# Whole gate and silu bursts on ScalarE in a scan kernel: where each stands among the decays

## The chip, the cores and the metric

One core of one Trainium2 chip runs the whole program. The metric is device time in microseconds (us), the median of several executions; 0.5% of it is 2.4 us.

## What is computed

A selective scan, four batches of 512 positions, 512 channels, 16 states, then a mixed linear layer. Cut to what matters:

```
x   = silu(causal_conv4(ctx @ in_proj.T) + conv_b)             # u, per batch 512 channels x 512 positions
dt  = softplus(dt_proj(x_proj(x)[:16]) + dt_b);  B, C = the other 32 rows of x_proj(x)
state = state * exp(dt * A) + (dt * x) * B      # a recurrence along the positions, 16 states
y   = sum_n(state * C) + D * x
x1  = x_in + y * silu(layernorm(x_in))           # the gate
out = x1 + layernorm(x1) @ sum_r(factors) / sqrt(8) + bias     # the FFN
```

## The kernel before

The work is 16 steps, `s` = 0 to 15: batch `b` = s // 4 and a block of 128 channels `k` = s % 4. A step has eight pairs `j` = 0 to 7, each two of the 16 states over 512 positions. A pair is written (s,j) below. Four engines work on a pair in turn:

- ScalarE (ACT) writes the decays exp(dt*A) of the pair into `dA`, two activations of 128x512 (`decay`, line 786). `dA` lies in PSUM and has two places, so the decays of pair j wait until pair j-2 has left its place (`decays`, just below it).
- GpSimd (POOL) writes dtu*B into `h`, a ring of eight pairs (`times_b`, line 1103), and at the end of a step `dtu` of the next one (line 1089).
- VectorE (DVE) scans the pair (`scan`, line 956) and multiplies by C (`times_c`, line 962). For the pairs that the table `POOL_C` names, the scan writes into `h`, not `dA`, and POOL multiplies, three pairs later (line 1096).
- TensorE (PE) adds the two states into `y` in PSUM (`state_sum`, line 528), in the order of `SUM_ORDERS`.

The order on each engine is written out by hand in `step(s)`: after the decays of pair j, ACT does whatever tables name slot j. ACT keeps one table set, for exp and ln. Softplus and silu need another, so each such burst is a table load, the work, and a load back. Softplus of the next step stands at `SOFTPLUS_SLOTS[s]`. The gate of a batch, four silu activations of 128x512 (line 700), is done in its first step in two halves at `GATE_SLOTS[b]`. The silu of the next batch's convolution, which writes `u` (line 692), is done in two pieces behind pair 4: three blocks in the second step of a batch, one in the third. `STATS_SLOTS` places two activations on layer norm statistics (lines 704, 710). `t_final_` (line 774) copies a finished FFN tile out of PSUM, `t_xnT_` (line 770) a transposed tile, both when PE has made them.

On DVE, `gate_y` (line 970) gates the previous step's y behind scan 1, `add_x1` (line 998) adds it to x1 behind scan 2 or 3, and three `conv_part`s (line 930) stand behind scans 6, 7 and 0 for blocks not convolved by PE.

Of the kernel before, what the change touches and what calls it, by code (L numbers as in the profile page):

```python
# [27 lines left out]
ACT = mybir.ActivationFunctionType  # L28
# [4 lines left out]
BATCH, L, DM = 4, 512, 256  # L33
DI, N, TAPS, RANK = 512, 16, 4, 16
KB = DI // P
# [21 lines left out]
TENSOR_CONV = (5, 6, 7, 8, 9)  # L57
SUM_ORDERS = {(0,): (1, 0, 2, 3, 4, 5, 6, 7), (0, 2): (1, 0, 3, 2, 4, 5, 6, 7), (0, 2, 4): (1, 0, 3, 2, 5, 4, 6, 7),
              (0, 4): (1, 0, 2, 3, 5, 4, 6, 7)}
POOL_C = ((0, 4), (0,), (0, 2), (0, 2), (0, 2), (0, 2), (0, 2), (0, 2, 4), (0, 2), (0, 2, 4), (0, 2), (0, 2, 4), (0, 2),  # L60
          (0, 2), (0, 2), (0, 2))
SOFTPLUS_SLOTS = (2, 2, 2, 2, 0, 2, 2, 2, 0, 2, 2, 2, 0, 2, 2, 2)
GATE_SLOTS = ((4, 6), (2, 5), (2, 5), (2, 5))
C_LAG = 3
STATS_SLOTS = (5, 3, 5, 3, 3, 3, 3, 3, 3, 3, 3, 3, 3, 3, 3, 3)
TENSOR_RESIDUAL = (0, 1, 2, 6, 8)
FIRST_FILL = (6, 0, 2, 2, 3)
IDLE_FILL = {(0, -1): 14, (0, 3): 3, (1, 3): 4, (3, 3): 4, (4, 1): 3, (5, 6): 2, (7, 6): 2, (8, 1): 2, (8, 6): 2, (9, 6): 2,
# [3 lines left out]
def build(nc, x, ctxT, w_inT, channel, x_projT, dt_wT, factors, bias, out):  # L72
    bc_dram = nc.dram_tensor("bc_scratch", (BATCH, 2 * N, L), F32, kind="Internal").ap()

    with ExitStack() as ctx:
# [33 lines left out]
        u = sb("u", [P, 2, KB, L])  # L109
        acc = sb("acc", [P, KB, L])  # L110
# [119 lines left out]
        def blocks_at(part, s, at):  # L230

            early = {t: ((t + KB, 5), (t + KB, 6), (t + KB, 7), (t + KB + 1, 1), (t + KB + 1, 4),
                         (t + KB + 2, -1), (t + KB + 2, 2)) for t in range(2 * KB)}
            for t in (KB - 2, 2 * KB - 2):
                early[t] = early[t][:FINAL] + ((t + KB + 2, 3),)
            early[KB - 1] = early[KB - 1][:EVAC] + ((2 * KB, 5),) + early[KB - 1][LAYER:]
            early[2 * KB - 1] = early[2 * KB - 1][:LAYER] + ((3 * KB, 5), (3 * KB + 1, 1))
            if part <= NORM:
                early.update(RAW_STATS)
            return [t for t, parts in early.items() if parts[part] == (s, at)]  # L240
# [418 lines left out]
        def _(act):  # L659
# [23 lines left out]
                act.wait_ge(conv, conv_count(k))  # L683
                act.activation(u[:, 0, k, :], acc[:, k, :], ACT.Silu).then_inc(u_done, 1)

            def silu_blocks(b, first, last):

                wait_conv(act, b * KB + last - 1)
                if b >= 2:
                    act.wait_ge(y_init, (b - 1) * KB)  # L690
                    act.wait_ge(d_dtu, (b - 1) * KB)
                act.activation(u[:, b % 2, first:last], acc[:, first:last], ACT.Silu).then_inc(u_done, last - first)

            def gate_half(b, half):

                act.wait_ge(g_nb, (b + 1) * KB)
                if b > 0:
                    act.wait_ge(gated, b * KB - 1 + half)
                for k in range(half * (KB // 2), (half + 1) * (KB // 2)):
                    act.activation(gate[:, k, :], x1_block(b, k), ACT.Silu, bias=g_r[:, 2, k:k + 1],  # L700
                                   scale=g_r[:, 1, k:k + 1]).then_inc(g_done, 1)

# [97 lines left out]
            def step(s):  # L800
                b, k = divmod(s, KB)

                nu = s + KB + 2
                is_u, is_g, is_d = nu < STEPS, b + 1 < BATCH, s + 1 < STEPS

                for j in range(PAIRS):
                    decays(s, k, j)

                    if s == KB + 1 and j in SCALE_SLOTS:
                        i = SCALE_SLOTS.index(j)  # L810
                        act.wait_ge(f_centred, i + 1)
                        act.activation(fsum[:, i, :], fsum[:, i, :], ACT.Copy, scale=FR ** -0.5).then_inc(f_scaled, 1)

                    if j == SOFTPLUS_SLOTS[s] and is_d:
                        act.preload_act_table_set("softplus")  # L815
                        softplus(s + 1)
                        act.preload_act_table_set("natural_log_exp_and_others")  # L817
                    if s == 0 and j == 0:
                        conv_tap(work0, KB)
                    if s == 0 and j == 1:  # L820
                        x_in_copy(work1, KB + 1)
                        lnv(g_r, g_mv, slice(0, KB), g_aggr, KB, g_lnv)
                        expv(g_r, slice(0, KB), g_lnv, 1, g_expv)
                        act.wait_ge(g_neg, 1)
                        for i in range(KB):
                            nb(g_r, g_mv, i, g_expv, 1, g_nb)
                    if s == KB and j == 7:
                        act.wait_ge(f_mean, 1)
                        act.activation(row_b[:], work1[:], ACT.Copy).then_inc(f_mean_evac, 1)
                    for t in blocks_at(FINAL, s, j):  # L830
                        t_final_(t)
                    if s == 0 and j == 5:
                        conv_out(KB + 1)
                    if j == 3 and s > 0 and s + KB + 1 in TENSOR_CONV:
                        conv_out(s + KB + 1)
                    if j == STATS_SLOTS[s] and is_g:
                        act.wait_ge(x_landed, (b + 2) * 16)
                        act.wait_ge(g_nb, (b + 1) * KB)
                        minus_mean(g_mv, b + 1, k, g_scratch, g_mean)
                    if j == 3 and s - 1 in TENSOR_RESIDUAL:  # L840
                        x1_evac(s - 1)
                    if k == 0 and j in GATE_SLOTS[b]:
                        act.preload_act_table_set("silu_and_others")
                        gate_half(b, GATE_SLOTS[b].index(j))
                        act.preload_act_table_set("natural_log_exp_and_others")
                    if j == 4 and k in (1, KB - 2) and b + 1 < BATCH:
                        act.preload_act_table_set("silu_and_others")
                        silu_blocks(b + 1, *((0, KB - 1) if k == 1 else (KB - 1, KB)))
                        act.preload_act_table_set("natural_log_exp_and_others")
                    if j == STATS_SLOTS[s] and is_g:  # L850
                        var_sum(g_mv, b + 1, k, g_scratch, g_mean, s + 1, g_var)
                    if j in (2 if s == STEPS - 1 else 4 if s == STEPS - 2 else 6 if s == STEPS - 3 else 5, 7):
                        for w in w_at(s)[j // 7:j // 7 + 1]:
                            w_copy(w)
                    for t in blocks_at(EVAC, s, j):
                        if is_g:
                            act.wait_ge(g_var, s + 1)
                        t_xnT_(t)
                    for t in blocks_at(MEAN, s, j):
                        act.wait_ge(x1_added, (t // KB + 1) * KB)  # L860
                        if t > 2 * KB:
                            act.wait_ge(t_var, t)
                        elif t > 0:
                            act.wait_ge(t_turned, t)
                        minus_mean(t_mv, t // KB, t % KB, xn[:], t_mean)
                    for t in blocks_at(VAR, s, j):
                        var_sum(t_mv, t // KB, t % KB, xn[:], t_mean, t + 1, t_var)
                    for t in blocks_at(NORM, s, j):
                        lnv(t_r, t_mv, slice(t % KB, t % KB + 1), t_var, t + 1, t_lnv, 1.0 / DI)
                        if t >= 2 * KB and t % KB == 0:  # L870
                            act.wait_ge(t_xn, 2 * KB)
                        expv(t_r, slice(t % KB, t % KB + 1), t_lnv, t + 1, t_expv)
                        if t >= 2 * KB:
                            continue
                        nb(t_r, t_mv, t % KB, t_expv, t + 1, t_nb)
                        t_xn_(t)
                    if j == 6 and k == KB - 1 and is_g:
                        lnv(g_r, g_mv, slice(0, KB), g_var, (b + 1) * KB, g_lnv, 1.0 / DI)
                        expv(g_r, slice(0, KB), g_lnv, b + 2, g_expv)
                        for i in range(KB):  # L880
                            nb(g_r, g_mv, i, g_expv, b + 2, g_nb)
                    if j == 6:
                        if is_u and nu in TENSOR_CONV:
# [350 lines left out]
```

## Time and profile before

| | |
|---|---|
| median of 3 runs | 481.11 us (479.55 to 481.75) |
| the profiled execution | 481.48 us, of which the profile's span is 479.7 us |
| TensorE clock granted, mean | 0.979 |
| PE / DVE / ACT / POOL busy | 91 / 94 / 76 / 90% of the span |
| chain that ended last, by engine | POOL 39%, DVE 18%, issue 18%, PE 15%, DMA 5%, ACT 3% |

The busy shares tell how much an engine works, not whether it is waited for. The chain names at each moment one engine that released the next work. The waits tell which engine sat idle until which other one was done.

### The profile page before, as it was taken

To read this page: it belongs to the slowest core of one execution; us is meant where nothing else is said; L and a number is where in the kernel's file an instruction comes from. 1 tells how busy PE (TensorE), PEld (TensorE's weight loads), DVE (VectorE), ACT (ScalarE), POOL (GpSimd) and SP (SyncE) were. 2 spreads that over 40 slices of the span, in tenths; PEclk is the share of its full clock that TensorE was granted. 3 is DMA by queue.
4 is the path that set the end of the run, shared out by engine and by line. 5 is a ranking of instruction groups with operands and counts; after the bars stand their busy time and mean duration, and the time that the engine had idled before them with its cause. 6 is when DMAs were issued, how large, how long until landed. Compare 5 with 4: busy or idle time off the path is not lost.

```text
span 479.7 us, 4156 instructions
## 1 busy us (share of the span) xinstructions
PE 438.1 (91%) x1119; PEld 187.4 (39%) x1132; DVE 451.2 (94%) x324; ACT 363.0 (76%) x595; POOL 429.4 (90%) x226
## 2 busy tenths in 40 slices
PE   8998798899999779899989798899989998989996
PEld 5242342434433243433434243343434443334432
DVE  5798899999999999999999997999998999999996
ACT  4678795887689798796899879697899876654422
POOL 4369999899999999997999979798999969999982
PEclk9999899999999969999999889999999999999999
DMA  5799746339992000100793000000495000000002
GB/s 193 260 350 359 198 81 142 51 78 217 292 362 77 1 0 0 53 15 0 239 412 122 0 23 0 1 23 0 118 396 237 1 22 23 22 22 22 2 0 88
DMA packets 16848, 53.97 MB, mean 113 GB/s; under 512 B 1828, under 2 KB 2084, under 8 KB 15800
## 3 DMA queue, kind: packets, MB, share of 16 engines
q1 hardware_dynamic: 15384, 45.14, 26.3%
q0 software_dynamic: 1152, 8.39, 8.7%
q8 instruction: 9, 0.15, 0.1%
q10 hardware_dynamic: 288, 0.18, 0.1%
q14 instruction: 15, 0.12, 0.1%
HBM read 49.24 MB, written 4.46 MB: 112 GB/s over the span
## 4 chain that ended last, share of the span: by engine, by line
POOL 39%; DVE 18%; issue 18%; PE 15%; DMA 5%; ACT 3%; SPq 2%; POOLq 0%; DVEq 0%
POOL h L1103 30%; DVE dA L956 12%; POOL h L1096 6%; PE y L528 6%; DMA b_rep<-bc_scratch 4%; DVE h L956 3%; DVE h L962 2%; PE work L406 2%; POOL dtu L1089 2%; PE work L516 1%; SPq L339 1%; ACT dA L786 1%; PE dA L432 1%; PE y L618 1%; SPq L334 1%
## 5 line engine op out<-in xcount | busy, mean ns | idle before, releaser
L1103 POOL TENSOR_TENSOR h<-b_rep,dtu 128x1024 f32<-128x1024 f32 x127 | 303.7, 2440 | 12.3 <-DMA b_rep<-bc_scratch 11.5
L528 PE MATMUL y<-h,ident 128*128 128x512 f32 x508 | 242.4, 615 | 30.9 <-DVE h L962 28.1
L956 DVE TENSOR_TENSOR_SCAN dA<-dA,h 128x1024 f32<-128x1024 f32 x94 | 214.9, 2287 | 13.8 <-ACT dA L786 13.3
L786 ACT ACTIVATE dA<-dt,a_neg 128x512 f32<-128x512 f32 x256 | 165.6, 680 | 76.2 <-DVE h L962 62.2
L528 PEld LDWEIGHTS y<-h,ident 128*128 128x128 f32 x508 | 94.6, 194 | 165.1 <-issue 107.2
L962 DVE TENSOR_TENSOR h<-dA,c_rep 128x1024 f32<-128x1024 f32 x93 | 113.4, 1219 | 2.1
L1096 POOL TENSOR_TENSOR h<-h,c_rep 128x1024 f32<-128x1024 f32 x34 | 81.4, 2394 | 13.5 <-DVE h L956 13.4
L956 DVE TENSOR_TENSOR_SCAN h<-dA,h 128x1024 f32<-128x1024 f32 x34 | 77.5, 2278 | 0.1
L516 PE MATMUL work<-fsum,xnT 128*128 128x512 f32 x64 | 28.8, 592 | 0.0
L406 PE MATMUL work<-ctx_sb,w_in 128*128 128x512 f32 x60 | 28.1, 598 | 0.3 <-DMA ctx_sb<-ctxT 0.3
L930 DVE SCALAR_TENSOR_TENSOR acc<-work,chan,acc 128x511 f32<-128x511 f32 (+2 forms) x30 | 21.6, 730 | 1.3 <-ACT acc L665 1.2
L1089 POOL TENSOR_TENSOR dtu<-dt,u 128x512 f32<-128x512 f32 x15 | 19.9, 1327 | 0.0
L817 ACT ACT_TABLE_LOAD x15 | 19.2, 1283 | 0.3
L815 ACT ACT_TABLE_LOAD x15 | 19.2, 1283 | 0.3
L516 PEld LDWEIGHTS work<-fsum,xnT 128*128 128x128 f32 x64 | 12.2, 190 | 15.3 <-issue 15.3
L418 PE MATMUL work<-row_b,x 128*128 128x512 f32 (+3 forms) x40 | 17.9, 591 | 0.0
L559 PE MATMUL y<-u,diag_d 128*128 128x512 f32 x32 | 17.4, 626 | 0.0
L439 PE MATMUL work<-dt_low,w_dt 32*128 32x512 f32 x30 | 16.8, 640 | 0.0
L406 PEld LDWEIGHTS work<-ctx_sb,w_in 128*128 128x128 f32 x60 | 10.9, 191 | 12.6 <-issue 11.0
L704 ACT ACTIVATE xnT<-x 128x512 f32<-128x512 f32 x13 | 8.0, 618 | 9.0 <-DVE x L991 9.0
L492 PE MATMUL work<-fsum,x 128*128 128x512 f32 x32 | 14.6, 598 | 0.0
L523 PE MATMUL y<-ones,still 128*128 128x512 bf16 x45 | 12.6, 385 | 0.6 <-issue 0.2
(130 smaller groups left out, 397.4 us busy)
## 6 DMA issues: line engine op xcount, KB each, us to landing
b_rep<-bc_scratch SPq DMA_DIRECT2D x32, 512.0 KB, 9.6
c_rep<-bc_scratch SPq DMA_DIRECT2D x32, 512.0 KB, 9.7
fsum<-factors POOLq DMA_DIRECT2D x8, 1024.0 KB, 8.1
x<-x SPq DMA_DIRECT2D x4, 1024.0 KB, 7.6
out<-x SPq DMA_DIRECT2D x16, 256.0 KB, 2.0
ctx_sb<-ctxT SPq DMA_DIRECT2D x3, 512.0 KB, 5.5
ctx_sb<-ctxT SPq DMA_DIRECT2D x2, 256.0 KB, 4.4
w_in<-w_inT SPq DMA_DIRECT2D x1, 384.0 KB, 5.2
```

The costliest lines, as they stand in the source:

```text
L406: mm = pe.matmul(bank[:], w_in[:, k, c, :], ctx_sb[:, c, :], start=(c == 0), stop=(c == CB - 1))
L516: pe.matmul(work1[:], xnT[:, k, :], fsum[:, k, :], start=(k == 0), stop=False)
L528: mm = pe.matmul(y[:], ident[:], h[:, (s * PAIRS + j) % H_RING, i, :], start=False, stop=(j == sum_order(s)[-1] and i == 1))
L786: act.activation(dA[:, j % 2, i, :], dt[:, k % 2, :], ACT.Exp, scale=a_neg[:, k, 2 * j + i:2 * j + i + 1]).then_inc(exp_done, 1)
L815: act.preload_act_table_set("softplus")
L817: act.preload_act_table_set("natural_log_exp_and_others")
L930: dve.scalar_tensor_tensor(out=acc[:, k, i:L], in0=bank[:, 0:L - i], scalar=cw[:, k, TAPS - 1 - i:TAPS - i], in1=acc[:, k, i:L], op0=ALU.m ...
L956: dve.tensor_tensor_scan(pair if on_pool(s * PAIRS + j) else decay, decay, pair, 0.0, ALU.mult, ALU.add).then_inc(scanned, 1)
L962: dve.tensor_tensor(h[:, (s * PAIRS + j) % H_RING], dA[:, j % 2], c_rep[:, j], ALU.mult).then_inc(mulc, 1)
L1089: pool.tensor_tensor(dtu[:, k % 2, :], dt[:, k % 2, :], u[:, n // KB % 2, k, :], ALU.mult).then_inc(d_dtu, 1)
L1096: pool.tensor_tensor(h[:, p % H_RING], h[:, p % H_RING], c_rep[:, p % PAIRS], ALU.mult).then_inc(pmulc, 1)
L1103: pool.tensor_tensor(h[:, (s * PAIRS + j) % H_RING], b_rep[:, j], dtu[:, k % 2, :].unsqueeze(1).to_broadcast([P, 2, L]), ALU.mult).then_in ...
```

## The change

Each batch's gate becomes one burst of four activations, each batch's silu one activation of 128x2048; `BURST_SLOTS` gives the slot of each. Seven bursts go, and with them 14 table loads. Gates stand in steps 0, 4, 8, 12 behind pairs 4, 2, 2, 4; silu in steps 2, 6, 10 behind pairs 4, 2, 2, in the last two ahead of the FFN copy. The whole gate waits for the gated y of the previous batch's third block at its start and of the fourth block ahead of its last activation. Softplus moves from slot 2 to 0 in steps 6 and 10, from 0 to 2 in step 12. Statistics move from slot 3 to 5 in steps 4 and 8 (entry 12 changes too, but step 12 has none). In steps 4 and 8 the second POOL product is pair 4, not 2, and step 11 gives one of its three POOL products, pair 4, to DVE.

```diff
-POOL_C = ((0, 4), (0,), (0, 2), (0, 2), (0, 2), (0, 2), (0, 2), (0, 2, 4), (0, 2), (0, 2, 4), (0, 2), (0, 2, 4), (0, 2),
+POOL_C = ((0, 4), (0,), (0, 2), (0, 2), (0, 4), (0, 2), (0, 2), (0, 2, 4), (0, 4), (0, 2, 4), (0, 2), (0, 2), (0, 2),
           (0, 2), (0, 2), (0, 2))
-SOFTPLUS_SLOTS = (2, 2, 2, 2, 0, 2, 2, 2, 0, 2, 2, 2, 0, 2, 2, 2)
-GATE_SLOTS = ((4, 6), (2, 5), (2, 5), (2, 5))
+SOFTPLUS_SLOTS = (2, 2, 2, 2, 0, 2, 0, 2, 0, 2, 0, 2, 2, 2, 2, 2)
+BURST_SLOTS = {0: 4, 2: 4, 4: 2, 6: 2, 8: 2, 10: 2, 12: 4}
-STATS_SLOTS = (5, 3, 5, 3, 3, 3, 3, 3, 3, 3, 3, 3, 3, 3, 3, 3)
+STATS_SLOTS = (5, 3, 5, 3, 5, 3, 3, 3, 5, 3, 3, 3, 5, 3, 3, 3)
...
-            def silu_blocks(b, first, last):
-
-                wait_conv(act, b * KB + last - 1)
+            def silu_batch(b):
+
+                wait_conv(act, b * KB + KB - 1)
                 if b >= 2:
                     act.wait_ge(y_init, (b - 1) * KB)
                     act.wait_ge(d_dtu, (b - 1) * KB)
-                act.activation(u[:, b % 2, first:last], acc[:, first:last], ACT.Silu).then_inc(u_done, last - first)
+                act.activation(u[:, b % 2], acc[:], ACT.Silu).then_inc(u_done, KB)
-            def gate_half(b, half):
+            def gate_batch(b):
                 act.wait_ge(g_nb, (b + 1) * KB)
-                if b > 0:
-                    act.wait_ge(gated, b * KB - 1 + half)
-                for k in range(half * (KB // 2), (half + 1) * (KB // 2)):
+                for k in range(KB):
+                    if b > 0 and k in (0, KB - 1):
+                        act.wait_ge(gated, b * KB - (1 if k == 0 else 0))
...
+                    if k == KB - 2 and b + 1 < BATCH and j == BURST_SLOTS[s] == 2:
+                        act.preload_act_table_set("silu_and_others")
+                        silu_batch(b + 1)
+                        act.preload_act_table_set("natural_log_exp_and_others")
                     for t in blocks_at(FINAL, s, j):
                         t_final_(t)
...
-                    if k == 0 and j in GATE_SLOTS[b]:
+                    if k == 0 and j == BURST_SLOTS[s]:
                         act.preload_act_table_set("silu_and_others")
-                        gate_half(b, GATE_SLOTS[b].index(j))
+                        gate_batch(b)
                         act.preload_act_table_set("natural_log_exp_and_others")
-                    if j == 4 and k in (1, KB - 2) and b + 1 < BATCH:
+                    if k == KB - 2 and b + 1 < BATCH and j == BURST_SLOTS[s] > 2:
                         act.preload_act_table_set("silu_and_others")
-                        silu_blocks(b + 1, *((0, KB - 1) if k == 1 else (KB - 1, KB)))
+                        silu_batch(b + 1)
                         act.preload_act_table_set("natural_log_exp_and_others")
```

ACT in step 6, from the softplus to the second of the two silu pieces before, and to the statistics behind the silu now (`u<-acc` is the silu, `dt<-work` the softplus, `dA<-dt` the decays, two of them a pair, `x<-work` the FFN copy):

```order
-L815 ACT_TABLE_LOAD
-L752 ACTIVATE dt<-work 128x512
-L817 ACT_TABLE_LOAD
-L774 ACTIVATE x<-work 128x512
-L786 ACTIVATE dA<-dt,a_neg 128x512 x2
-L704 ACTIVATE xnT,g_mv<-x 128x512
-L710 ACTIVATE xnT,g_mv<-x,g_mv 128x512
-L786 ACTIVATE dA<-dt,a_neg 128x512 x2
-L847 ACT_TABLE_LOAD
-L692 ACTIVATE u<-acc 128x512
-L849 ACT_TABLE_LOAD
```

```order
+L786 ACTIVATE dA<-dt,a_neg 128x512 x2
+L815 ACT_TABLE_LOAD
+L752 ACTIVATE dt<-work 128x512
+L817 ACT_TABLE_LOAD
+L786 ACTIVATE dA<-dt,a_neg 128x512 x4
+L831 ACT_TABLE_LOAD
+L692 ACTIVATE u<-acc 128x2048
+L833 ACT_TABLE_LOAD
+L774 ACTIVATE x<-work 128x512
```

The softplus burst now stands behind pair 0, and the whole silu takes its former place behind pair 2; behind pair 4 no burst is left.

DVE in step 4, from the scan of pair 1 to that of pair 5, before and now (`h<-dA,c_rep` is a product on DVE; a scan whose result is `h` leaves its product to POOL):

```order
L956 SCALAR_TENSOR_TENSOR dA<-dA,h 128x1024
L970 TENSOR_TENSOR yg<-y,gate 128x512
L962 TENSOR_TENSOR h<-dA,c_rep 128x1024
L956 SCALAR_TENSOR_TENSOR h<-dA,h 128x1024
L998 TENSOR_TENSOR x<-work,x 128x4x128
L956 SCALAR_TENSOR_TENSOR dA<-dA,h 128x1024
L962 TENSOR_TENSOR h<-dA,c_rep 128x1024
L956 SCALAR_TENSOR_TENSOR dA<-dA,h 128x1024
L962 TENSOR_TENSOR h<-dA,c_rep 128x1024
L956 SCALAR_TENSOR_TENSOR dA<-dA,h 128x1024
```

```order
L960 SCALAR_TENSOR_TENSOR dA<-dA,h 128x1024
L974 TENSOR_TENSOR yg<-y,gate 128x512
L966 TENSOR_TENSOR h<-dA,c_rep 128x1024
L960 SCALAR_TENSOR_TENSOR dA<-dA,h 128x1024
L1002 TENSOR_TENSOR x<-work,x 128x4x128
L966 TENSOR_TENSOR h<-dA,c_rep 128x1024
L960 SCALAR_TENSOR_TENSOR dA<-dA,h 128x1024
L966 TENSOR_TENSOR h<-dA,c_rep 128x1024
L960 SCALAR_TENSOR_TENSOR h<-dA,h 128x1024
L960 SCALAR_TENSOR_TENSOR dA<-dA,h 128x1024
```

One product more stands between the scans of pairs 2 and 3, one less between those of 4 and 5 (lines are four later in the changed file).

## Rows read from the trace of the kernel before

**Rows 1.** The page: busy us, share of the span, instructions of each engine.

```profile
PE 438.1 (91%) x1119; PEld 187.4 (39%) x1132; DVE 451.2 (94%) x324; ACT 363.0 (76%) x595; POOL 429.4 (90%) x226
```

**Rows 2.** Waits: engine and line, awaited; us in total, times, longest.

```profile
PE y L528 <- DVE h L962: 28.1, 24, 3.0
...
POOL h L1096 <- DVE h L956: 13.4, 7, 3.1
DVE dA L956 <- ACT dA L786: 13.3, 13, 3.2
```

**Rows 3.** Timeline of DVE, scans after idle time: start, us, work, [idle <-awaited].

```profile
44.84 2.30 DVE L956 TENSOR_TENSOR_SCAN dA<-dA,h 128x1024 f32<-128x1024 f32 x1 [1.16 <-ACT dA L786]
54.03 2.30 DVE L956 TENSOR_TENSOR_SCAN dA<-dA,h 128x1024 f32<-128x1024 f32 x1 [2.17 <-ACT dA L786]
74.68 2.30 DVE L956 TENSOR_TENSOR_SCAN dA<-dA,h 128x1024 f32<-128x1024 f32 x1 [0.60 <-ACT dA L786]
...
156.54 2.30 DVE L956 TENSOR_TENSOR_SCAN dA<-dA,h 128x1024 f32<-128x1024 f32 x1 [0.50 <-ACT dA L786]
181.84 2.30 DVE L956 TENSOR_TENSOR_SCAN dA<-dA,h 128x1024 f32<-128x1024 f32 x1 [0.95 <-ACT dA L786]
...
268.51 2.30 DVE L956 TENSOR_TENSOR_SCAN dA<-dA,h 128x1024 f32<-128x1024 f32 x1 [0.99 <-ACT dA L786]
286.02 2.30 DVE L956 TENSOR_TENSOR_SCAN dA<-dA,h 128x1024 f32<-128x1024 f32 x1 [0.53 <-ACT dA L786]
294.93 2.30 DVE L956 TENSOR_TENSOR_SCAN dA<-dA,h 128x1024 f32<-128x1024 f32 x1 [3.16 <-ACT dA L786]
...
361.94 2.30 DVE L956 TENSOR_TENSOR_SCAN dA<-dA,h 128x1024 f32<-128x1024 f32 x1 [1.32 <-ACT dA L786]
380.10 2.30 DVE L956 TENSOR_TENSOR_SCAN dA<-dA,h 128x1024 f32<-128x1024 f32 x1 [0.99 <-ACT dA L786]
```

**Rows 4.** Timeline of ACT, a half gate in step 0.

```profile
39.37 1.28 ACT L843 ACT_TABLE_LOAD   x1
40.67 1.52 ACT L700 ACTIVATE gate<-x,g_r 128x512 f32<-128x512 f32 x2
```

**Rows 5.** The silu's line: duration ns min/median/max, starts, forms.

```profile
L692 ACT ACTIVATE u<-acc x6: 630/1057/1489, 70.5 to 319.0; 128x1536 f32<-128x1536 f32 x3, 128x512 f32<-128x512 f32 x3
```

**Rows 6.** Timelines of ACT and DVE, decays and scan of (2,5).

```profile
98.75 1.30 ACT L786 ACTIVATE dA<-dt,a_neg 128x512 f32<-128x512 f32 x2
...
100.28 2.29 DVE L956 TENSOR_TENSOR_SCAN dA<-dA,h 128x1024 f32<-128x1024 f32 x1
```

**Rows 7.** Timelines of ACT and DVE, decays and scan of (4,3).

```profile
144.21 1.30 ACT L786 ACTIVATE dA<-dt,a_neg 128x512 f32<-128x512 f32 x2
...
145.57 2.29 DVE L956 TENSOR_TENSOR_SCAN dA<-dA,h 128x1024 f32<-128x1024 f32 x1
```

**Rows 8.** The page: the products on DVE, busy us and mean ns.

```profile
L962 DVE TENSOR_TENSOR h<-dA,c_rep 128x1024 f32<-128x1024 f32 x93 | 113.4, 1219 | 2.1
```

**Rows 9.** Timeline of PE: step 8 to 9, step 11.

```profile
272.63 3.78 PE L528 MATMUL y<-h,ident 128*128 128x512 f32 x4 [3.04 <-DVE h L962]
...
290.04 0.60 PE L473 MATMUL work<-ident,xn 128*128 128x128 f32 x4
...
345.91 1.98 PE L528 MATMUL y<-h,ident 128*128 128x512 f32 x4 [0.49 <-DVE h L962]
```

**Rows 10.** Timelines of ACT and DVE, decays and scan of (6,3).

```profile
200.57 1.29 ACT L786 ACTIVATE dA<-dt,a_neg 128x512 f32<-128x512 f32 x2
...
202.78 2.28 DVE L956 TENSOR_TENSOR_SCAN dA<-dA,h 128x1024 f32<-128x1024 f32 x1
```

**Rows 11.** Timeline of DVE, the scan of (12,5).

```profile
375.57 2.29 DVE L956 TENSOR_TENSOR_SCAN dA<-dA,h 128x1024 f32<-128x1024 f32 x1
```

**Rows 12.** Timeline of POOL in step 13.

```profile
396.74 1.27 POOL L1147 TENSOR_TENSOR x<-x,row_b 128x512 f32<-128x512 f32 x1 [4.99 <-ACT xn L710]
```

**Rows 13.** Stages: us; busy of PE, PEld, DVE, ACT, POOL; granted clock; DMA.

```profile
271.65:278.48 6.83, 5.63 (x7) 2.50 (x9) 6.83 (x5) 3.59 (x6) 4.05 (x2) 0.50 0.00 0
```

## The prediction

> **What bounds the kernel now.** I read the busy shares first [rows 1]: DVE is busy 451.2 of 479.7 us, more than any other. The waits [rows 2] say what takes the rest. In the middle of the program DVE loses time almost only to ACT: 13 scans wait 13.3 us in all for decays. POOL, though it heads the chain, waits for scans seven times, 13.4 us in all and up to 3.1 at once, so it runs ahead of DVE most of the time, and PE waits 28.1 us for DVE's products. So DVE sets the pace and an idle microsecond of DVE is one of the span, as long as POOL and PE keep up. The DVE timeline then places the waits [rows 3]: ten of the 13, 12.4 us together. Eight of them follow a gate or silu burst. The other two are 286.02, where ACT itself had waited for PE, and 361.94, behind the softplus at slot 0 of step 12. With two places in `dA`, ACT is at most two pairs ahead, and a burst longer than that lead reaches DVE.
>
> **Lengths of the bursts.** A half gate holds ACT for a load of 1.28, two silus in 1.52 and a load back, 4.1 us [rows 4]. A whole gate is 1.5 more: 5.65. Silu takes 0.63 for one block and 1.49 for three [rows 5], 0.43 per further block, so 1.92 for four, and the burst 4.5 us, 1.3 more than the one-block piece. Fourteen loads and seven bursts go, 14 x 1.28 = 18 us of ACT; ACT at 76% does not need them, so only the DVE waits count.
>
> The Trainium skill, ScalarE: Activation LUTs, section What ACT_TABLE_LOAD costs, has 2.66 us for every switch, 1283 ns of load and some 1380 of drain. By it the change would take 14 x 2.66 = 37 us off ACT. The trace agrees with the first part and shows no second: the activation starts 1.30 us after its load [rows 4].
>
> **The sum, step by step.** Gains are waits that end; a loss is the new length less the lead that the scan's decays had. Times are of the trace before.
>
> - Step 0. The burst behind pair 6 goes: +2.17 (54.03). The one behind pair 4 grows by 1.52, and pair 5 had no lead (44.84, idle 1.16 already): -1.5. Net +0.65.
> - Step 1. The three-block silu goes: +0.6 (74.68).
> - Step 2. The silu grows by 1.3 behind pair 4. The decays of (2,5) end at 100.05, the scan starts at 100.28 [rows 6]: 0.23 of lead, so -1.1.
> - Step 4. The second half goes: +0.5 (156.54). The first grows by 1.52. The moved POOL product puts a product of 1.22 us on DVE [rows 8], 1.13 between starts, ahead of scan (4,3), and takes one away at pair 4. Before, the decays of (4,3) ended at 145.51 and the scan started at 145.57 [rows 7]. Now they end at 145.51 + 1.52 = 147.03, and DVE is free at 145.57 + 1.13 = 146.70: -0.35 with the hand-over, and +0.15 since a scan whose product is POOL's is followed closer. Statistics in slot 5 take 1.5 of the 3.9 us that the half gate leaves there. Net +0.3.
> - Step 5. The three-block silu goes: +0.95 (181.84). The transposed tile's copy waits for PE there, but leaves the decays 0.4 ahead of the scan.
> - Step 6. Softplus leaves slot 2 for slot 0, where pair 1 had 1.4 us of lead and the decays are then 0.8 early: nothing. The whole silu, 4.5 in place of 3.2, delays decays (6,3), which started at 200.57 and took 1.30, by 1.3 against a lead of 0.9 [rows 10]: -0.4. The end of the burst behind pair 4 yields nothing, as no scan waited there.
> - Step 8. As step 4, but the lead is 0.5, which covers it: +0.99 (268.51), +0.1: +1.1.
> - Step 9. The three-block silu goes, and the wait of 3.16 (294.93) was the largest. What is late next is PE: it is busy without a pause from 276.6 on, transposes the tile at 290.04 to 290.64 [rows 9], and ACT must copy that (0.5) ahead of the decays (1.3): they end at 292.5 where DVE is free at 291.77. A wait of 0.75 stays: +2.4. The wait of 0.53 at 286.02, also for PE, stays.
> - Step 10. As step 6: -0.4.
> - Step 11. One product comes from POOL to DVE: -1.15 between starts [rows 8]. POOL loses 2.4 us of work it had, no gain, as DVE sets the pace.
> - Step 12. The softplus at slot 2 ends the wait at 361.94: +1.32. The gate's second half goes: +0.99 (380.10). The whole gate behind pair 4: the scan of (12,0) ends at 360.62, decays (12,2) then take 1.3, the softplus burst 3.2, decays (12,3) 1.3, an FFN copy 0.5 and decays (12,4) 1.3 to 368.3, the gate ends at 373.95, the tile's copy at 374.45, decays (12,5) at 375.75, where DVE, 1.32 early, is ready at 375.57 - 1.32 = 374.25 [rows 11]: -1.5. Net +0.85.
>
> Sum: 0.65 + 0.6 - 1.1 + 0.3 + 0.95 - 0.4 + 1.1 + 2.4 - 0.4 - 1.15 + 0.85 = 3.8 us. In step 13 POOL waits 4.99 us for a statistic of ACT [rows 12] and then leads DVE by little. That statistic stands behind decays that wait for DVE, so ACT, POOL and DVE arrive there earlier by the same 3.8.
>
> The gated-y wait inside the whole gate costs nothing: `gate_y` stands behind scan 1, two silus ahead of the last one. The later u of step 2 is ready at about 97.5 in new time, x_proj on PE started at 100.03. DMAs are issued as before, none waits for anything later than it did by more than 1.3 us, and b_rep is on the path only at the program's start.
>
> The profiled execution took 481.48, and 3.8 less is 477.7; the median of 481.11 less 3.8 gives **477.3 us**, which I forecast.
>
> Bounds: terms with little lead (steps 2, 4, 6, 8, 10, 12) may each be off by some 0.3. Step 9 lies between 1.0, if PE falls another 1.4 behind, and 3.16 + 0.53 = 3.7, if PE is not in the way. The sum so lies between 1.5 and 6. I take 2.4 for step 9, since PE's own row gives it.
>
> **Rivals.**
>
> *PE keeps its clock at the step from 8 to 9.* PE idled 3.04 us ahead of 272.63 [rows 9], and just about there its granted clock fell to 1.2 GHz: 0.50 in the stretch of 271.65 to 278.48 [rows 13]. Now product (8,6) comes 1.1 us earlier against PE's work, and PE idles 1.9 us. If the clock stays at 2.4 GHz, PE is some 3 us earlier at the transposition, and the 0.75 and the 0.53 go too: 477.3 - 1.3 = 476.0. For it: the shorter idle. Against: another fall before, in step 0, followed an idle of only 1.9.
>
> *PE becomes the bound.* In steps 10 and 11 PE works for some 39 us up to 345.91 with no pause over 0.1, and then waits for DVE only 0.49 [rows 9]. If it is late by more than DVE gained, because its sums now come in other orders in steps 4, 8 and 11, what step 9 gives is handed back through the y that `gate_y` waits for: 477.3 + 2.4 = 479.7, no difference that can be told, which is within 2.4 us (0.5%). Against: no DVE row but one at the program's end waits for PE.
>
> *PE's clock falls where a burst now stands.* In step 0 the product of pair 5 comes 1.5 later, in step 2 that of pair 5 1.1 later, in step 12 that of pair 5 when PE has little else. [...] A fall like that one makes PE half as fast for 6.83 us [rows 13], 3.4 us lost, which DVE feels in full where PE has no slack left. Two, in steps 2 and 12, cost 6.8 and give 477.3 + 6.8 = 484.1, slower than before. The Trainium skill, TensorE: Matmul & The Clock Gate, section HAM oscillation, tells of a kernel that goes back to the slow clock at every wait for data. Against: in both places PE has a backlog, and its waits there were under 1.5 us.
>
> That the change does not do what it says is excluded by the order of instructions shown above.
>
> **Chances.** The sum as worked out, 0.47; PE's clock kept, 0.20; PE the bound, 0.20; clock falls, 0.06; the rest, 0.07, for a gain over 6 us or something unseen. Faster by over 0.5%, under 478.7: nearly all of the first two and a little of the rest, 0.69. Within 0.5%: 0.25. Slower by over 0.5%, over 483.5: 0.06. The range, 474.8 to 480.4, runs from the clock case with 1.2 us more (bounds of the small terms) to the PE case with 0.7 more, and leaves out the falls.
>
> **What would show it.** The DVE waits for ACT should drop from 13.3 to about 7 us: none left near 54, 75, 181 and 361; new ones of about 2.7 at (0,5), 1.1 at (2,5), 0.4 at (6,3) and (10,3), 1.5 at (12,5); 0.75 at (9,5). ACT's busy time should fall by some 18 us with 14 loads fewer, DVE's rise by 1.2. POOL's waits for scans should shrink. A wait of DVE for PE or POOL in steps 1 to 12 would be the second rival's mark, a granted clock of 0.50 in step 3 or 13 the third's. The forecast is wrong in kind if DVE's waits fall as told and the span does not.

## The result and the profile after

| | before | changed |
|---|---|---|
| median, 9 executions each | 481.0 us (479.55 to 483.71) | 476.52 us (475.69 to 478.75) |
| the profiled execution | 481.48 | 478.26 |
| its span | 479.7 | 476.5 |
| scan (0,4) to scan (15,7), start to start | 465.11 - 41.40 = 423.71 | 461.91 - 43.62 = 418.29 |

The ratio is 0.9911, with a 95% interval of 0.9887 to 0.9935: faster by 0.9%, some 4.3 us. Forecast was 477.3, in a range of 474.8 to 480.4.

The last row of the table is the measure used from here on, called the stretch. It leaves out the start of the program, which differs between executions. In the changed profile DVE waited there for a C row:

```profile
39.02 1.23 DVE L966 TENSOR_TENSOR h<-dA,c_rep 128x1024 f32<-128x1024 f32 x1 [1.14 <-DMA c_rep<-bc_scratch]
...
43.62 2.28 DVE L960 TENSOR_TENSOR_SCAN h<-dA,h 128x1024 f32<-128x1024 f32 x1
```

So the scan of (0,4) began 2.2 us later than before, and the 3.2 us between the two spans are 5.4 us won behind it, less 2.2 lost ahead of it. The change did not bring that loss: in a second profile of the changed kernel (last table of the experiments) the scan of (0,4) began at 40.83 us, 2.8 earlier, and the stretch was the same to 0.08 us.

The page's busy times (engine, us, share of the span, instructions), which answer to [rows 1]:

```profile
PE 434.6 (91%) x1119; PEld 186.9 (39%) x1132; DVE 452.3 (95%) x325; ACT 344.7 (72%) x578; POOL 425.1 (89%) x225
```

ACT fell by 18.3 us, 18.0 of them 14 loads of 1.28, and DVE rose by 1.1, the product of step 11. The waits (engine and line, awaited; us, times, longest), which answer to [rows 2]:

```profile
PE y L528 <- DVE h L966: 25.4, 23, 1.8
...
POOL h L1100 <- DVE h L960: 9.2, 6, 2.1
DVE dA L960 <- ACT dA L786: 7.2, 10, 2.6
```

DVE's waits for decays fell from 13.3 to 7.2 us, POOL's waits for scans from 13.4 to 9.2. The DVE timeline names the ten, which answer to [rows 3]:

```profile
48.47 2.30 DVE L960 TENSOR_TENSOR_SCAN dA<-dA,h 128x1024 f32<-128x1024 f32 x1 [2.57 <-ACT dA L786]
102.03 2.30 DVE L960 TENSOR_TENSOR_SCAN dA<-dA,h 128x1024 f32<-128x1024 f32 x1 [1.00 <-ACT dA L786]
140.63 2.30 DVE L960 TENSOR_TENSOR_SCAN dA<-dA,h 128x1024 f32<-128x1024 f32 x1 [0.29 <-ACT dA L786]
148.71 2.30 DVE L960 TENSOR_TENSOR_SCAN dA<-dA,h 128x1024 f32<-128x1024 f32 x1 [0.16 <-ACT dA L786]
203.44 2.30 DVE L960 TENSOR_TENSOR_SCAN dA<-dA,h 128x1024 f32<-128x1024 f32 x1 [0.36 <-ACT dA L786]
236.97 2.30 DVE L960 TENSOR_TENSOR_SCAN dA<-dA,h 128x1024 f32<-128x1024 f32 x1 [0.52 <-ACT dA L786]
...
291.11 2.30 DVE L960 TENSOR_TENSOR_SCAN dA<-dA,h 128x1024 f32<-128x1024 f32 x1 [0.34 <-ACT dA L786]
312.49 2.30 DVE L960 TENSOR_TENSOR_SCAN dA<-dA,h 128x1024 f32<-128x1024 f32 x1 [0.36 <-ACT dA L786]
338.47 2.30 DVE L960 TENSOR_TENSOR_SCAN dA<-dA,h 128x1024 f32<-128x1024 f32 x1 [0.28 <-ACT dA L786]
373.47 2.30 DVE L960 TENSOR_TENSOR_SCAN dA<-dA,h 128x1024 f32<-128x1024 f32 x1 [1.34 <-ACT dA L786]
```

They are (0,5), (2,5), (4,1), (4,3), (6,3), (7,5), (9,5), (10,3), (11,3) and (12,5). Those behind halves and pieces that no longer exist are gone. The one at (9,5), 3.16 before, is 0.34, and that at (9,3), 0.53 before, is gone.

PE between steps 8 and 9, which answers to [rows 9]:

```profile
268.29 3.70 PE L528 MATMUL y<-h,ident 128*128 128x512 f32 x8 [1.28 <-DVE h L966]
272.26 1.99 PE L528 MATMUL y<-h,ident 128*128 128x512 f32 x4 [0.27 <-DVE h L966]
276.23 1.98 PE L528 MATMUL y<-h,ident 128*128 128x512 f32 x4 [1.55 <-DVE h L966]
...
288.60 0.60 PE L473 MATMUL work<-ident,xn 128*128 128x128 f32 x4
```

In place of one idle time of 3.04 us there are three of 1.28, 0.27 and 1.55. The tile that ACT copies ahead of the decays of (9,5), turned at 288.60 here, is turned 12.51 us behind the start of scan (9,0) in place of 13.57. In the stage of 264 to 290 (columns as in [rows 13], which it answers to) the granted clock is 1.00 throughout, 2.4 GHz, not 0.50:

```profile
264.00:290.00 26.00, 22.84 (x62) 10.16 (x63) 25.93 (x18) 20.50 (x39) 24.63 (x12) 1.00 0.03 10
```

### The profile page after: what moved, and what is told of

The parts are those of the page before. It is cut to its first block, busy times and chain, and to the rows that moved or that the text cites. A ratio compares the mean times of both kernels' runs of the same rounds, so it can differ in the third digit from the quotient of the medians.

```text
span 476.5 us, 4131 instructions
## 1 busy us (share of the span) xinstructions
PE 434.6 (91%) x1119; PEld 186.9 (39%) x1132; DVE 452.3 (95%) x325; ACT 344.7 (72%) x578; POOL 425.1 (89%) x225
## 4 chain that ended last, share of the span: by engine, by line
POOL 38%; issue 21%; DVE 18%; ACT 10%; PE 7%; DMA 5%; SPq 1%; POOLq 0%; DVEq 0%; ACTq 0%
POOL h L1107 28%; DVE dA L960 13%; POOL h L1100 7%; ACT dA L786 3%; DVE h L960 3%; PE y L528 2%; DMA c_rep<-bc_scratch 2%; POOL dtu L1093 2%; PE work L406 2%; DVE h L966 2%; ACT gate L700 1%; DMA w_in<-w_inT 1%; DMA ctx_sb<-ctxT 1%; PE dA L432 1%; ACT L815 1%
## 5 line engine op out<-in xcount | busy, mean ns | idle before, releaser
L528 PE MATMUL y<-h,ident 128*128 128x512 f32 x508 | 238.2, 607 | 29.3 <-DVE h L966 25.4
L960 DVE TENSOR_TENSOR_SCAN dA<-dA,h 128x1024 f32<-128x1024 f32 x95 | 217.1, 2286 | 7.7 <-ACT dA L786 7.2
L528 PEld LDWEIGHTS y<-h,ident 128*128 128x128 f32 x508 | 93.5, 191 | 160.9 <-issue 105.9
L966 DVE TENSOR_TENSOR h<-dA,c_rep 128x1024 f32<-128x1024 f32 x94 | 114.6, 1219 | 3.1 <-DMA c_rep<-bc_scratch 1.1
L1100 POOL TENSOR_TENSOR h<-h,c_rep 128x1024 f32<-128x1024 f32 x33 | 79.9, 2422 | 11.2 <-DVE h L960 9.2
L960 DVE TENSOR_TENSOR_SCAN h<-dA,h 128x1024 f32<-128x1024 f32 x33 | 75.2, 2278 | 0.1
L406 PE MATMUL work<-ctx_sb,w_in 128*128 128x512 f32 x60 | 29.4, 621 | 1.7 <-DMA ctx_sb<-ctxT 1.5
```

Of the source, the lines that this page charges most:

```text
L406: mm = pe.matmul(bank[:], w_in[:, k, c, :], ctx_sb[:, c, :], start=(c == 0), stop=(c == CB - 1))
L528: mm = pe.matmul(y[:], ident[:], h[:, (s * PAIRS + j) % H_RING, i, :], start=False, stop=(j == sum_order(s)[-1] and i == 1))
L960: dve.tensor_tensor_scan(pair if on_pool(s * PAIRS + j) else decay, decay, pair, 0.0, ALU.mult, ALU.add).then_inc(scanned, 1)
L966: dve.tensor_tensor(h[:, (s * PAIRS + j) % H_RING], dA[:, j % 2], c_rep[:, j], ALU.mult).then_inc(mulc, 1)
L1100: pool.tensor_tensor(h[:, p % H_RING], h[:, p % H_RING], c_rep[:, p % PAIRS], ALU.mult).then_inc(pmulc, 1)
```

## The experiments

Eleven runs follow, of ten kernels: the changed kernel ran once more, and one version twice. The executions of one kernel spread over 2 to 7 us, so each run is read by the stretch of its one profile first and its time second. A ratio is always to the kernel before as it ran on the same chip; its median there was 481.2 to 482.9 us, so medians of different sections are not to be subtracted. "Step n" below is the time from the start of scan (n,0) to that of (n+1,0), against the same in the kernel before (step 0 from (0,4)).

### The gates back in halves

```diff
-SOFTPLUS_SLOTS = (2, 2, 2, 2, 0, 2, 0, 2, 0, 2, 0, 2, 2, 2, 2, 2)
+SOFTPLUS_SLOTS = (2, 2, 2, 2, 0, 2, 0, 2, 0, 2, 0, 2, 0, 2, 2, 2)
+GATE_SLOTS = ((4, 6), (2, 5), (2, 5), (2, 5))
-STATS_SLOTS = (5, 3, 5, 3, 5, 3, 3, 3, 5, 3, 3, 3, 5, 3, 3, 3)
+STATS_SLOTS = (5, 3, 5, 3, 3, 3, 3, 3, 3, 3, 3, 3, 3, 3, 3, 3)
...
-                    if k == 0 and j == BURST_SLOTS[s]:
+                    if k == 0 and j in GATE_SLOTS[b]:
-                        gate_batch(b)
+                        gate_half(b, GATE_SLOTS[b].index(j))
```

with `gate_half` as before and entries 4 and 8 of `POOL_C` at (0, 2).

> The gates go back to two halves, in the slots they had before, with the softplus of step 12, the statistics and the POOL products of steps 4 and 8 that belong to them; silu stays whole. Theory A (only bursts longer than the decays' lead count): the waits of DVE in steps 0, 4, 8 and 12 come back, in the sum 0.65 + 0.3 + 1.1 + 0.85 = 2.9, with what the changed kernel's trace shows in those steps (0.84, 0.48, 1.22, 1.07) 3.6 us slower than the change: about 479.5 to 480.1. Stretch from the start of scan (0,4) to that of (15,7): 423.7 us before, 418.3 changed, here about 421.9. Theory B (ACT's saved time counts as such, 5.4 us of the stretch for 14 loads, 0.39 a load): eight loads come back, 3.1 us, so this run alone does not separate; the places of the waits do, at (0,5) 1.2 and (0,7) 2.2. Theory C (the gain came from TensorE's clock between steps 8 and 9): whatever the gates do, the time follows whether the clock falls there.

Measured: stretch 420.86; median 480.24 us (12 executions), ratio to before 0.9958 (0.993 to 0.9985). The waits are back where they were, 1.16 and 2.17 us in step 0 and 0.99 at (8,6), and steps 0, 4 and 8 are again as long as before. Step 12 is not: it stayed 1.03 us shorter, which is the miss of 1.0 us in the expected stretch. The wait at (12,1), behind the softplus in slot 0, was 1.32 us before and is 0.29 here:

```profile
361.43 2.30 DVE L961 TENSOR_TENSOR_SCAN dA<-dA,h 128x1024 f32<-128x1024 f32 x1 [0.29 <-ACT dA L787]
```

The product that step 11 gave to DVE delays DVE by 1.28 us, but the table load of this softplus by 0.26 only, so most of the softplus is covered. The gate part as a whole is worth 420.86 - 418.29 = 2.57 us on top of the rest.

This run bears on the clock as well. In its timeline PE idled 3.04 us at the same place, and in the stage around it (the stage's fence, columns as in [rows 13]) its clock stayed at 1.00:

```profile
274.87 1.98 PE L529 MATMUL y<-h,ident 128*128 128x512 f32 x4 [3.04 <-DVE h L967]
```

```profile
271.00:290.00 19.00, 14.40 (x41) 6.41 (x40) 18.97 (x14) 15.34 (x28) 15.58 (x7) 1.00 0.04 14
```

### Silu back in pieces

```diff
-SOFTPLUS_SLOTS = (2, 2, 2, 2, 0, 2, 0, 2, 0, 2, 0, 2, 2, 2, 2, 2)
+SOFTPLUS_SLOTS = (2, 2, 2, 2, 0, 2, 2, 2, 0, 2, 2, 2, 2, 2, 2, 2)
...
+                    if b in PIECES and j == 4 and k in (1, KB - 2):
+                        act.preload_act_table_set("silu_and_others")
+                        silu_blocks(b + 1, *((0, KB - 1) if k == 1 else (KB - 1, KB)))
+                        act.preload_act_table_set("natural_log_exp_and_others")
```

with PIECES = (0, 1, 2), the batches for which this replaces the whole silu.

> Silu goes back to two pieces behind pair 4 of the second and third step of a batch, with softplus in slot 2 of steps 6 and 10; the gates stay whole. Theory A: waits come back at (1,5) 0.7, (5,5) 0.95 and (9,5) 3.2, those at (2,5), (6,3) and (10,3) go. By the terms of the changed trace 0.69 + 1.05 + 3.45 - 1.09 - 0.45 - 0.45 = 3.2 us slower than the change (2.0 by my own sum): 478.5 to 479.7; stretch 421.5. Theory B (0.39 us a load, six loads): 2.3 us slower. Theory C: slower only if the clock falls between steps 8 and 9.

Measured: stretch 420.48, 1.0 us less than expected; median 478.07 us (9), ratio 0.9928 (0.9903 to 0.9954). Waits of 0.61 at (1,5) and 0.95 at (5,5) are back, those at (2,5), (6,3) and (10,3) are gone. But (9,5) waits 2.90, not 3.16, and (9,3) does not wait:

```profile
234.38 2.30 DVE L973 TENSOR_TENSOR_SCAN dA<-dA,h 128x1024 f32<-128x1024 f32 x1 [0.34 <-ACT dA L795]
291.08 2.30 DVE L973 TENSOR_TENSOR_SCAN dA<-dA,h 128x1024 f32<-128x1024 f32 x1 [2.90 <-ACT dA L795]
```

Step 9 is 0.90 us shorter than before with no silu moved in it. So of the 3.46 us that step 9 gained in the change, 0.9 is not the silu's. The whole silu is then worth 420.48 - 418.29 = 2.19 us; the sum of the prediction gave its terms 2.05.

### The third POOL product of step 11 kept

```diff
-POOL_C = ((0, 4), (0,), (0, 2), (0, 2), (0, 4), (0, 2), (0, 2), (0, 2, 4), (0, 4), (0, 2, 4), (0, 2), (0, 2), (0, 2),
+POOL_C = ((0, 4), (0,), (0, 2), (0, 2), (0, 4), (0, 2), (0, 2), (0, 2, 4), (0, 4), (0, 2, 4), (0, 2), (0, 2, 4), (0, 2),
```

> The change with the third POOL product of step 11 kept. Theory A: DVE has one product less, 1.28 us faster than the change (about 475.2; stretch 417.0), since POOL's lead at (12,0), 6.2 us, pays the 2.4 + 1.3 that this takes of it. Rival: POOL, head of the chain with 38%, falls behind in steps 12 and 13, DVE waits for it, and the time is that of the change or worse (476.5 to 477.7).

Measured: stretch 417.18; median 475.63 us (6), ratio 0.9857 (0.982 to 0.9895). Step 11 is as long as before, and step 12 keeps its 1.07 us. POOL's least lead over a scan in step 12 is 2.5 us. POOL did not become late; this part of the change costs 1.1 us of the stretch and is not needed with the rest of it.

### The POOL products of steps 4 and 8 back

```diff
-POOL_C = ((0, 4), (0,), (0, 2), (0, 2), (0, 4), (0, 2), (0, 2), (0, 2, 4), (0, 4), (0, 2, 4), (0, 2), (0, 2), (0, 2),
+POOL_C = ((0, 4), (0,), (0, 2), (0, 2), (0, 2), (0, 2), (0, 2), (0, 2, 4), (0, 2), (0, 2, 4), (0, 2), (0, 2), (0, 2),
```

> The change with the second POOL product of steps 4 and 8 back at pair 2. Work of DVE and POOL is the same, only what covers the whole gate differs. Theory A: scans (4,3) and (8,3) come 1.13 us earlier of themselves and wait for decays that do not: waits of 0.16 + 1.13 + about 0.1 = 1.4 at (4,3) and about 1.0 at (8,3), 2.3 us slower than the change in all, 478.8; stretch 420.6. Rival (the place of a product is indifferent, the number counts): 476.5.

Measured: stretch 420.72; median 478.26 us (9), ratio 0.9929 (0.9903 to 0.9956). The two waits:

```profile
145.95 2.30 DVE L960 TENSOR_TENSOR_SCAN dA<-dA,h 128x1024 f32<-128x1024 f32 x1 [1.29 <-ACT dA L786]
...
257.40 2.30 DVE L960 TENSOR_TENSOR_SCAN dA<-dA,h 128x1024 f32<-128x1024 f32 x1 [0.89 <-ACT dA L786]
```

The same work in another order costs 2.4 us. A product on DVE between the burst and the next scan is cover, behind that scan it is none.

### The kernel before, with PE kept busy behind step 8

```diff
-IDLE_FILL = {(0, -1): 14, (0, 3): 3, (1, 3): 4, (3, 3): 4, (4, 1): 3, (5, 6): 2, (7, 6): 2, (8, 1): 2, (8, 6): 2, (9, 6): 2,
+IDLE_FILL = {(0, -1): 14, (0, 3): 3, (1, 3): 4, (3, 3): 4, (4, 1): 3, (5, 6): 2, (7, 6): 2, (8, 1): 2, (8, 5): 6, (8, 6): 2, (9, 6): 2,
```

(Six matmuls with a matrix of zeros as weights, which add nothing to y, behind the sixth sum of step 8.)

> The kernel before, with six further filling matmuls on zeros behind the sixth sum of step 8, where TensorE idled 3.04 us and its clock then fell to 1.2 GHz. Theory D (1 us of what step 9 gained beyond the sum is TensorE's clock and not the silu): the clock stays at 2.4 GHz behind step 8, the wait of 0.53 at (9,3) goes and that at (9,5) shrinks to about 2.9, step 9 is 0.9 us shorter and all other steps as before: stretch 422.8, time 1 us less than before. Rival (the copy in step 9 is late for another reason, or the gain in step 9 is all silu): waits of 0.53 and 3.16 stay, stretch 423.7.

Measured: stretch 422.82, step 9 shorter by 0.89 us, every other step within 0.02 of before. The six fills shorten the idle time from 3.04 to 1.75 us (timeline of PE, then that of DVE), and the clock stays at 1.00 (stage, third fence):

```profile
272.19 1.98 PE L528 MATMUL y<-h,ident 128*128 128x512 f32 x4 [1.75 <-DVE h L962]
```

```profile
293.60 2.30 DVE L956 TENSOR_TENSOR_SCAN dA<-dA,h 128x1024 f32<-128x1024 f32 x1 [2.91 <-ACT dA L786]
```

```profile
269.00:290.00 21.00, 17.65 (x54) 8.33 (x54) 20.97 (x15) 17.31 (x28) 17.54 (x8) 1.00 0.03 13
```

The profile confirms what a kept clock is worth in step 9, 0.89 us, the same as with silu back in pieces (0.90). It does not show that the fills kept the clock, since with the gates in halves it stayed at 1.00 behind 3.04 us of idle time without them. The times show no gain: the median is 482.51 us (12 executions, 480.13 to 485.22), ratio 1.0009 (0.9981 to 1.0037). An effect of 0.2% is below what they can tell.

### Softplus left behind pair 2, in front of the whole silu

```diff
-SOFTPLUS_SLOTS = (2, 2, 2, 2, 0, 2, 0, 2, 0, 2, 0, 2, 2, 2, 2, 2)
+SOFTPLUS_SLOTS = (2, 2, 2, 2, 0, 2, 2, 2, 0, 2, 2, 2, 2, 2, 2, 2)
```

> The change with softplus of steps 6 and 10 left in slot 2, so that softplus and the whole silu stand in a row behind pair 2. Theory A: the 3.2 us of softplus come on top of a lead that is used up already (0.36 of wait): waits of 0.36 + 3.2 = 3.55 at (6,3) and (10,3), 6.4 us slower than the change in all, stretch 424.7, time about 483. TensorE then idles some 3 us in these steps and its clock may fall, up to 1 us more each. Rival (a burst is absorbed over the following pairs, as DVE has 5% of idle time): under 2 us slower.

Measured: stretch 428.68, 10.4 us over the change where 6.4 were expected; median 485.88 us (10), ratio 1.0074 (1.0039 to 1.011), slower than before. The waits at (6,3) and (10,3) are 3.56 us each, to 0.01 as forecast. A fall of the clock was forecast as possible, at up to 1 us in each of the two steps; 4.0 us came on top. They are new waits of 1.50 at (6,7) and 0.93 at (7,3), and larger ones at (7,5), 0.78, and (11,3), 1.39. The PE timeline of step 6, a stage of it, and the timelines of ACT and of DVE show where that at (6,7) comes from:

```profile
207.49 3.78 PE L406 MATMUL work<-ctx_sb,w_in 128*128 128x512 f32 x4 [3.75 <-DMA ctx_sb<-ctxT]
```

```profile
207.00:213.00 6.00, 5.51 (x7) 2.42 (x8) 5.97 (x4) 4.05 (x8) 5.92 (x5) 0.50 0.00 0
```

```profile
217.73 0.59 ACT L741 ACTIVATE dt_low<-work 32x512 f32<-32x512 f32 x1 [3.77 <-PE work L432]
```

```profile
220.15 2.30 DVE L960 TENSOR_TENSOR_SCAN dA<-dA,h 128x1024 f32<-128x1024 f32 x1 [1.50 <-ACT dA L786]
```

The FFN copy stands behind both bursts. The copy ended at 202.97; the SP queue issued the store of the finished tile at 203.00 and the load of the next ctx behind it, at 203.43. So the copy's delay becomes the load's, and PE waits 3.75 us for that load. Its clock falls to 0.50. The sums and x_proj are then late, ACT waits 3.77 us for x_proj, and DVE for ACT. In the kernel before PE waited 0.29 us there for the load, in the changed one 1.50. What the late load costs and what the slow clock costs on top is not separated.

This run and the one with the POOL products of steps 4 and 8 back also decide against the plain rival that ACT's saved time counts as such, at 0.39 us a load. By the totals alone that rival holds up: 3.1 us forecast for the gates and 2.57 measured, 2.3 for silu and 2.19 measured. But moving two products cost 2.43 us and moving two softplus bursts 10.4 us, with not one table load more or less.

### One silu alone

The kernel before with the last batch's silu whole in step 10, and softplus of step 10 in slot 0.

```diff
-SOFTPLUS_SLOTS = (2, 2, 2, 2, 0, 2, 2, 2, 0, 2, 2, 2, 0, 2, 2, 2)
+SOFTPLUS_SLOTS = (2, 2, 2, 2, 0, 2, 2, 2, 0, 2, 0, 2, 0, 2, 2, 2)
...
+                    if s == 10 and j == 2:
+                        act.preload_act_table_set("silu_and_others")
+                        silu_batch(b + 1)
+                        act.preload_act_table_set("natural_log_exp_and_others")
...
-                    if j == 4 and k in (1, KB - 2) and b + 1 < BATCH:
+                    if j == 4 and k in (1, KB - 2) and b + 1 < BATCH - 1:
```

> The kernel before with a single edit, the largest term alone: the silu of the last batch whole, behind pair 2 of step 10, softplus of step 10 in slot 0. Theory A: the wait at (9,5) falls from 3.16 to 0.75 if TensorE's clock falls behind step 8 and to 0.34 (and 0.53 at (9,3) goes too) if it stays; a wait of 0.36 at (10,3) comes. Stretch 423.7 - 2.4 + 0.45 = 421.7, or 423.7 - 3.45 + 0.45 = 420.7 with the clock kept; 0.4 to 0.6% faster than before. Rival (the terms are not independent, TensorE is late in steps 10 and 11): under 1 us faster.

Measured: stretch 423.32; median 481.33 us (12), ratio 0.997 (0.9935 to 1.0005). This run missed the expected stretch for a fallen clock by 1.6 us, and its gain of 0.4 us is what the rival gave (under 1 us). The rival's reason was not found: steps 10 and 11 are 0.46 longer, as forecast, and as long as before. Its DVE timeline, and the stage between steps 8 and 9:

```profile
76.76 2.30 DVE L968 TENSOR_TENSOR_SCAN dA<-dA,h 128x1024 f32<-128x1024 f32 x1 [1.31 <-ACT dA L794]
...
289.04 2.30 DVE L968 TENSOR_TENSOR_SCAN dA<-dA,h 128x1024 f32<-128x1024 f32 x1 [1.47 <-ACT dA L794]
295.57 2.30 DVE L968 TENSOR_TENSOR_SCAN dA<-dA,h 128x1024 f32<-128x1024 f32 x1 [0.77 <-ACT dA L794]
```

```profile
273.00:283.00 10.00, 7.55 (x11) 2.88 (x13) 10.00 (x8) 6.38 (x12) 6.52 (x3) 0.66 0.00 0
```

The wait at (9,5) is 0.77 us, as the sum had it for a fallen clock (0.75), and that at (10,3) 0.36. But the clock fell a little later than in the profile before, with 1.47 in place of 0.53 us at (9,3), and there was a low stretch from 57.5 to 64.3 us too, into step 1, where (1,5) waits 1.31, not 0.60. Against the kernel before, step 9 won 1.45 us and step 1 lost 0.70. So the two waits that belong to the moved silu came as forecast, but no gain is shown by this run's time; what an execution's clock adds moves the stretch by over 1 us.

### The change again, and two versions built on it

The better version keeps the third POOL product of step 11 (as above) and does the second batch's silu in its two pieces (PIECES = (0,)).

> A version meant to beat both: the change, with POOL's third product kept in step 11 (worth 1.28 us in the run before) and the silu of the second batch in its two pieces in steps 1 and 2, as before (the wait at (2,5) of 1.0 goes, that at (1,5) of 0.6 to 0.7 comes: 0.4 less). Theory A: stretch 418.3 - 1.3 - 0.4 = 416.7, time 1.7 us less than the change, 1.3% less than before. Rival: POOL becomes late, stretch over 417.2.

Measured: stretch 416.56; median 474.89 us (6), ratio 0.9847 (0.9815 to 0.9878). The three kernels below then ran on one chip: the change,

> The changed kernel itself, once more, beside the two below on one chip. Theory A and D: what differs between executions lies outside the placing of the bursts, in the start (when the first B and C rows land) and in falls of TensorE's clock; so the stretch from scan (0,4) to (15,7) is 418.3 again, up to 1.5 more where the clock falls in a step whose decays wait for TensorE (1, 5, 7, 9), and all DVE waits stand where they stood. Time 0.9% under before.

the better version,

> The best version so far (third POOL product of step 11 kept, silu of the second batch in two pieces) again, beside the change on one chip: stretch 416.6, 1.7 us less than the change, and some 1.3 to 1.5% under before.

and the better version with (0, 2, 4) for step 10 too.

> The best version so far with a third POOL product in step 10 too. Theory A: a further 1.28 us less, stretch 415.3, if POOL keeps its lead. It takes 3.7 us of lead (2.4 of POOL's work, 1.3 of DVE's), and the least lead in step 12 is 2.5 us. Some of the 3.4 us that POOL waits for scans in steps 11 and 12 give way, so I expect a lead near 0 and 0.5 to 1.3 us gained. Rival: POOL, now in front nowhere from step 11 on, sets the end: waits of DVE for POOL in step 12 and no gain.

| | stretch | median of 6 | ratio to before |
|---|---|---|---|
| the change | 418.37 | 475.97 | 0.9876 (0.9846 to 0.9905) |
| the better version | 417.04 | 475.42 | 0.9854 (0.9825 to 0.9883) |
| with step 10 too | 416.26 | 474.11 | 0.9831 (0.9804 to 0.9858) |

The ratios are a little lower than that of the first nine executions, 0.9911, whose interval the change's overlaps. The change's stretch repeats to 0.08 us. The better version's first stretch was 416.56, its second 417.04: the wait at (7,5), for a tile that PE must turn first, was 0.44 and 0.78. The third product of step 10 shortens step 10 by 1.28 us and gives 0.87 back in step 11: not to POOL, whose least lead in step 12 is still 1.3 us, but to PE, whose work DVE now overtakes. ACT waits 0.88 us for PE's FFN tile in front of the decays of (11,3):

```profile
333.24 0.60 ACT L783 ACTIVATE x<-work 128x512 f32<-128x512 f32 x1 [0.88 <-PE work L519]
```

```profile
335.06 2.30 DVE L973 TENSOR_TENSOR_SCAN dA<-dA,h 128x1024 f32<-128x1024 f32 x1 [1.15 <-ACT dA L795]
```

Both versions beat the kernel before clear of noise, and by stretch the change too, by 1.3 to 2.1 us. By their times the intervals of the three overlap. The third product of step 10 brings 0.3 to 0.8 us of stretch over the two profiles of the better version, where 0.5 to 1.3 was expected.

## Why the prediction was right, point by point

- **What bounds the kernel.** Right. Where a DVE wait for ACT was taken away, it came off the stretch in full; behind the start, DVE waited for POOL at (13,4) alone, 0.48 us, as before (0.50).
- **The number.** 477.3 us forecast, 476.52 measured. That they lie so close is in part luck: the profile did not take the path that the sum took through step 9, and beside the kernel before on another chip the change's ratio was 0.9876, 1.2% and not 0.9. The range held because it took in the rival with the clock kept (476.0).
- **The sum.** 3.8 us forecast, 5.4 in the stretch of the profile, 4.5 between the medians. By steps, forecast and found: 0, +0.65 and +0.86; 1, +0.6 and +0.70; 2, -1.1 and -1.10; 4, +0.3 and +0.49; 5, +0.95 and +1.05; 6, -0.4 and -0.45; 8, +1.1 and +1.23; 9, +2.4 and +3.46; 10, -0.4 and -0.45; 11, -1.15 and -1.28; 12, +0.85 and +1.07. Step 7, for which I forecast nothing, lost 0.18, by a longer wait at (7,5). Put together from the runs: the whole silu 2.2, the kept clock 0.9, the whole gates of steps 0, 4 and 8 2.6, and steps 11 and 12 together 0.2 lost, about 5.4 in all.
- **The small misses.** Each wait that goes gives some 0.1 us more than its length. A scan that did not wait starts 0.08 us ahead of its predecessor's end in the record, one that waited does not. I read idle times for gains and left that overlap out; with eight waits gone that is an estimated 0.65 of the 1.6 us missed. The product of step 11 was sized from the distance of 1.15 between starts. The whole of it is 1.28, because the scan loses with it the closer follow-up of a scan whose product is POOL's (2.20 us from scan to scan, not 2.33), which I had counted in step 4 and not here.
- **Step 9.** The term that was too small. The step of the reasoning that failed is that PE transposes the tile at 290.04 whatever happens. The rival "PE keeps its clock at the step from 8 to 9" is what came about in the profile, at 0.20 against 0.47. It too was sized wrong: PE was to be some 3 us earlier at the tile and was 1.06 earlier (12.51 us behind scan (9,0), not 13.57), so 0.34 of wait is left at (9,5), and the clock was worth 0.9 us, not 1.3. The kernel before with the fills shows that worth with nothing else moved. The forecast wait of 0.75 was right for a fallen clock: the run with one silu moved has 0.77. When the clock falls is open: in the run with gates in halves it stayed after the same 3.04 us of idle time.
- **Steps 4 and 8.** The lead was weighed to 0.2 us: 0.35 forecast at (4,3) and 0.16 found, none at (8,3), as forecast. The run with the products put back shows that they are what pays for the whole gate.
- **Step 12.** I gave the moved softplus +1.32. It is true of the move by itself: with the product of step 11 kept on POOL, step 12 wins 1.07 all the same. But the run with gates in halves shows that the product which step 11 gives to DVE yields 1.03 there without the move; together they yield it once. So the two edits were not independent, and one of them was for nothing.
- **PE becomes the bound.** Did not come about in the change. Its mark appeared in the last version, where a third product in step 10 was two thirds handed back in step 11.
- **The clock falls where a burst stands.** Did not come about at (2,5) or (12,5): PE had no idle time over 1.5 us in steps 2 and 12 of the changed kernel. With softplus and silu in a row the clock fell in steps 6 and 10. That kernel was slower than before, by 5.0 us of the stretch: the expected cost of the row alone makes 1.0 of them, the late load and the clock the rest.
- **The table load.** Fourteen loads of 1.283 us are 18.0 of the 18.3 us that ACT lost; most of the rest is the silu in one activation. The Trainium skill's 2.66 us for every switch (ScalarE: Activation LUTs, What ACT_TABLE_LOAD costs) would have made it 37. The traces of before and after do not agree: but for the first one, a load starts 0.02 us behind the activation ahead of it, and the next activation starts 1.30 us behind the load's start where it waits for nothing else.

## What to carry to other kernels

A burst on an engine that feeds another through two buffers costs its length less the lead it meets, so merging bursts pays only where the whole one meets a lead. Count the lead at the very pair, and count what can be moved into it: one product placed ahead of the scan, not behind it, was worth 1.28 us in step 4 and 1.14 in step 8. Look for what else queues behind the burst. Here it was a copy of half a microsecond that a store, a load, a matmul and its clock hung on.

## What the runs showed that was not expected

- The same idle time of PE of 3.04 us at the same place was followed by a clock of 1.2 GHz in the profiles of the kernel before and of the one with a single silu moved, and not in that with gates in halves. In step 9 a fall cost 0.9 us of the stretch in the kernel before and 2.0 in the one with a single silu moved (step 9 shorter by 1.45 in place of 3.45). The second began 1.2 us after the idle time, the first 1.0 us before its end, so more of PE's work was slow in the second: it turned the tile of step 9 at 14.52 us behind scan (9,0), against 13.57.
- Not every fall costs. All thirteen profiles have a low stretch in step 5, of 3.4 to 10.2 us, and its length does not matter there: it was 10.2 us in the kernel before and 3.4 with silu back in pieces, and step 5 was the same to 0.01 us.
- In the thirteen profiles scan (0,4) began between 40.8 and 43.8 us after the span's start, with the same instructions ahead of it. The two profiles of the changed kernel differ by 2.7 us in their spans, and all of it is the start (40.83 against 43.62). Whether start and clock make up the whole spread between executions is not shown, as each run has one profile. Steps compared between profiles agreed to some hundredths of a microsecond, but for steps 7 and 13 and some with a fall, where medians could not tell half a per cent.
